# An adaLN block with routed attention on one core: a second set of slot orders, statistics spread over slots, keys of four heavy batches made early, and two banks for the last transposes

## The reference, cut to what matters

```
h = layernorm(x) * (1 + ca) + sa
x = x + ga * attention(h)                    # causal, one head of 128
h = layernorm(x) * (1 + cb) + sb
x = x + gb * ffn(h)
ffn(h):                                      # 8 heads of 64
    light = local_attention(rmsnorm(h))      # windows of 128 tokens, output projection
    s_q, s_kv = h @ q_token, h @ kv_token    # one score per token
    idx_q  = top 128 of 50 steps of coordinate descent on s_q
    idx_kv = top 256 of the same on s_kv
    q from rows idx_q, keys and values from rows idx_kv, values times their scores
    heavy = softmax(q k^T) v, projected, times the query scores
    return light, with heavy added at rows idx_q
```

## Time and profile before

| | us |
|---|---|
| median of 3 runs (480.55 to 482.89) | 482.2 |
| the profiled execution | 482.58 |
| its span, first to last instruction | 480.7 |
| PE busy | 445.8 (93%) |
| DVE busy | 328.1 (68%) |
| ACT busy | 345.6 (72%) |
| POOL busy | 267.3 (56%) |

### The profile page before, as it was taken

How to read it: one execution, slowest core, us unless ns; L and a number is a source line. 1 busy time by engine, 2 the same in 40 slices (tenths; PEclk the granted TensorE clock), 3 DMA queues, 4 the chain that set the end, 5 groups by cost and what they waited for, 6 DMA issues and landing times.

```text
span 480.7 us, 12054 instructions
## 1 busy us (share of the span) xinstructions
PE 445.8 (93%) x4088; PEld 393.3 (82%) x4088; DVE 328.1 (68%) x1099; ACT 345.6 (72%) x1260; POOL 267.3 (56%) x325
## 2 busy tenths in 40 slices
PE   7858889999999999899997799999999999999994
PEld 6747688998989988787786688888888888888873
DVE  5874788778768897989879964555555454555551
ACT  3665989889788877677775678667776766677761
POOL 3147576576576776332332335544666666556555
PEclk9996999999999999999999999999999999999998
DMA  6880000001001001000000000100000010000002
GB/s 219 237 314 22 14 13 13 13 1 33 25 1 35 23 20 49 3 12 13 12 12 13 6 8 24 35 18 7 12 11 13 12 18 14 16 12 13 7 8 22
DMA packets 20108, 16.28 MB, mean 34 GB/s; under 512 B 1968, under 2 KB 18880, under 8 KB 19792
## 3 DMA queue, kind: packets, MB, share of 16 engines
q1 hardware_dynamic: 16480, 13.01, 8.8%
q0 software_dynamic: 2816, 2.10, 3.3%
q10 hardware_dynamic: 752, 0.40, 0.3%
HBM read 10.23 MB, written 5.28 MB: 32 GB/s over the span
## 4 chain that ended last, share of the span: by engine, by line
PE 64%; DVE 14%; ACT 5%; issue 4%; POOL 4%; POOLq 0%; ACTq 0%; DVEq 0%
PE bank L905 6%; PE bank L916 6%; PE bank L660 6%; PE bank L931 6%; PE bank L662 5%; PE bank L661 5%; PE bank L813 4%; PE bank L854 4%; PE bank L843 4%; PE bank L827 4%; ACT pr L591 3%; PE bank L872 3%; DVE cd_min L1208 3%; PE bank L944 3%; DVE nmx L1162 2%
## 5 line engine op out<-in xcount | busy, mean ns | idle before, releaser
L420 POOL TENSOR_TENSOR pr<-pr,rinv 128x512 f32<-128x512 f32 x64 | 66.5, 1040 | 84.2 <-DVE rinv L1168 84.2
L432 POOL TENSOR_TENSOR pr<-pr,rinv 128x512 f32<-128x512 f32 x64 | 72.7, 1155 | 63.8 <-DVE rinv L1313 63.8
L591 ACT ACTIVATE pr<-bank,nmx 128x128 f32<-128x128 f32 x256 | 90.5, 377 | 20.8 <-DVE nmx L1162 20.7
L634 ACT ACTIVATE pr<-bank,nmx 128x256 f32<-128x256 f32 x128 | 59.3, 485 | 19.3 <-DVE nmx L1307 19.3
L1307 DVE TENSOR_REDUCE nmx<-bank 128x2 f32<-128x512 f32 x64 | 41.9, 681 | 33.4 <-PE bank L905 33.4
L644 ACT ACTIVATE pt<-bank 128x512 f32<-128x512 f32 x64 | 38.2, 596 | 27.0 <-PE bank L916 27.0
L591 ACT ACTIVATION_READ_ACCUMULATOR pr<-bank,nmx 128x1 f32 x256 | 55.5, 217 | 0.0
L1162 DVE TENSOR_REDUCE nmx<-bank 128x4 f32<-128x512 f32 x64 | 42.8, 672 | 8.5 <-PE bank L813 8.4
L827 PE MATMUL bank<-ident,pr 128*128 128x128 f32 x256 | 38.9, 275 | 7.4 <-POOL pr L420 6.8
L916 PE MATMUL bank<-ident,pr 128*128 128x128 f32 x256 | 38.8, 274 | 1.6 <-ACT pt L644 1.6
L827 PEld LDWEIGHTS bank<-ident,pr 128*128 128x128 f32 x256 | 29.6, 141 | 10.6 <-POOL pr L420 8.5
(11 more groups left out here) (218 smaller groups left out, 1315.8 us busy)
## 6 DMA issues: line engine op xcount, KB each, us to landing
mod_bc<-mod_rows_scratch SPq DMA_DIRECT2D x1, 2560.0 KB, 15.4
X<-in_L_attn_x SPq DMA_DIRECT2D x4, 512.0 KB, 8.0
xh_scratch<-xhs SPq DMA_DIRECT2D x16, 128.0 KB, 1.9
out<-X SPq DMA_DIRECT2D x16, 128.0 KB, 1.8
mod_bc<-mod_rows_scratch SPq DMA_DIRECT2D x1, 1024.0 KB, 7.8
wkv_raw<-in_L_ffn_wkv_light SPq DMA_DIRECT2D x1, 512.0 KB, 7.6
mod_bc<-mod_rows_scratch SPq DMA_DIRECT2D x1, 512.0 KB, 3.8
wmod_sb<-in_L_wmod ACTq DMA_DIRECT2D x1, 384.0 KB, 5.3
```

The costliest lines, as they stand in the source:

```text
L420: pool.tensor_tensor(q, q, rinv[u][:, :, None].broadcast_to([P, 4, P]), ALU.mult)\
L432: pool.tensor_tensor(q, q, rinv[u][:, 0:2, None].broadcast_to([P, 2, N]), ALU.mult)\
L591: act.activation(pr[u][:, i * P:(i + 1) * P], ps[bank][:, i * P:(i + 1) * P], ACT.Exp, bias=nmx[u][:, i:i + 1], accum_out=sums[u][:, i:i + ...
L634: act.activation(pr[u][:, i * N:(i + 1) * N], ps[bank][:, i * N:(i + 1) * N], ACT.Exp, bias=nmx[u][:, i:i + 1], accum_out=sums[u][:, i:i + ...
```

## The change

In the first 18 slots each engine but SP now walks a list of its own (`HEAD = 18`); the list for the other slots is changed too. `A_AT` is written out with the same numbers. In the second list most H entries of PE, ACT and DVE keep their order inside the slot.

The statistics of one batch are taken per slot, in slots 3 to 6, 13 to 16 and 22 to 25; the small operations follow in the last slot of each four, 1/std one slot after that and the bias two. `h_transpose` of batch 4 is preceded by eight `keep_busy` transposes.

The keys of heavy batches 0 to 3 are made in slots 67 to 74, one half (six matmuls) a slot, into bank 5; ACT copies them into rows of `mod_bc` that are no longer read. Both stand first in their slot. The projections and both evacuations of these batches in phase H go, and their scores read `mod_bc`.

For the last heavy batch units 1 and 3 are transposed into bank 1 and copied out by DVE; units 0 and 2 stay with bank 4 and ACT. Its reciprocal of unit 3 stands ahead of the evacuation of the batch before. POOL's scatter moves from lag 19 to lag 17 and behind the last `normalise_h` in its slot.

```diff
-A_AT = [5 * b // 2 for b in range(B)]
+A_AT = [0, 2, 5, 7, 10, 12, 15, 17, 20, 22, 25, 27, 30, 32, 35, 37]
+HEAD = 18
-def run_slots(stages):
+def run_slots(head, stages=None):
     for t in range(END):
-        for phase, lag, f, *unit in stages:
+        for phase, lag, f, *unit in head if t < HEAD or stages is None else stages:
...
-        STATS_AT = (4, 11, 19)
+        STATS_AT = (3, 13, 22)
+        KEPT = 4
+        KEPT_AT = [SCORES_AT + 18 + i for i in range(2 * KEPT)]
+        LAST_PT_BANKS = (4, 1)
...
-                       ("H", 1, gather), ("A", 11, xhat), ("A", 7, ln2_rstd), ("H", 19, scatter), ("L", 15, add_light),
+                       ("H", 17, scatter), ("L", 3, normalise, 0)])
...
+            def kept_evac(t):
+                if t in KEPT_AT:
+                    n = KEPT_AT.index(t)
+                    act.wait_ge(hv["keptp"], n + 1)
+                    act.activation(mod_bc[:, 2 * n:2 * n + 2, 0:2, :].rearrange("p c j d -> p c (j d)"),
+                                   ps[5][:, :].rearrange("p (c t) -> p c t", c=2), ACT.Copy).then_inc(hv["kept"], 1)
             def k_evac_h(b):
-                act.wait_ge(hv["kp"], 2 * b + 1)
+                if b < KEPT:
+                    return
+                act.wait_ge(hv["kp"], 2 * (b - KEPT) + 1)
...
             def pt_evac_h(b, u):
+                if b == B - 1 and u % 2:
+                    return
...
-                if b in (0, 2):
+                if b in (0, 2, 4):
                     keep_busy(8)
...
+            def project_kept(t):
+                if t in KEPT_AT:
+                    n = KEPT_AT.index(t)
+                    pe.wait_ge(a["xlo"], B)
+                    at_least(pe, hv["kept"], n)
+                    project_half(5, KH_w, n % 2, n // 2).then_inc(hv["keptp"], 1)
             def project_kh_0(b):
+                if b < KEPT:
+                    return
...
             def p_transpose_h(b, u):
+                bank = 4
+                if b == B - 1:
+                    bank = LAST_PT_BANKS[u % 2]
+                    if u % 2:
+                        at_least(pe, hv["PTd"], u // 2)
+                    else:
+                        pe.wait_ge(hv["PT"], 4 * b + u // 2)
...
             def late_stats(t):
-                if t in STATS_AT:
-                    stats1(1 + STATS_AT.index(t))
-                    mean_var1(1 + STATS_AT.index(t))
+                for n, first in enumerate(STATS_AT):
+                    if first <= t < first + 4:
+                        b = 4 * (n + 1) + t - first
+                        stats1(b, b + 1)
+                    if t == first + 3:
+                        mean_var1(n + 1)
...
+            def pt_evac_last(b, u):
+                if b == B - 1:
+                    dve.wait_ge(hv["PTp"], 4 * b + u + 1)
+                    dve.wait_ge(hv["Op"], b)
+                    dve.tensor_copy(pt[u][:, :], ps[LAST_PT_BANKS[1]][:, :]).then_inc(hv["PTd"], 1)
```

More of the change, by code:

```diff
@@ L231, in adaln_routed_attention @@
         hv = {n: sem("h_" + n) for n in (
[L232 to L233 removed]
+            "xg0", "xg1", "keptp", "kept", "xqp", "xq", "qp", "q", "kp", "ka", "kd", "vp", "v", "Sp", "mx", "p", "ri", "pn",
+            "PTp", "PT", "PTd", "Op", "oT", "outp", "fin", "out0", "out1")}
         block = ctx.enter_context(nc.Block())
@@ L894, in scores_h, with keys @@
                 pe.wait_ge(hv["q"], b + 1)
-                pe.wait_ge(hv["ka"], b + 1)
-                pe.wait_ge(hv["kd"], b + 1)
+                if b == 0:
+                    pe.wait_ge(hv["kept"], 2 * KEPT)
+                    pe.wait_ge(lt["vd"], B)
+                if b < KEPT:
+                    at_least(pe, hv["v"], 2 * b)
+                else:
+                    pe.wait_ge(hv["ka"], b - KEPT + 1)
+                    pe.wait_ge(hv["kd"], b - KEPT + 1)
+                def keys(rows, c):
+                    if b < KEPT:
+                        return mod_bc[rows, 4 * b + c, 0:2, :].rearrange("p j d -> p (j d)")
+                    return KT[b % 2][rows, c, :]
                 for n in range(2):
@@ L905, in scores_h @@
                             mm = pe.matmul(ps[SCORE_BANKS[n][i]][:, m * N:(m + 1) * N], QT[b % 2][rows, c, 0:NQ],
-                                           KT[b % 2][rows, c, :], start=True, stop=True)
+                                           keys(rows, c), start=True, stop=True)
                     mm.then_inc(hv["Sp"], 1)
@@ L913, in p_transpose_h @@
                     pe.wait_ge(lt["oTd"], B)
-                at_least(pe, hv["PT"], g)
+                bank = 4
+                if b == B - 1:
+                    bank = LAST_PT_BANKS[u % 2]
+                    if u % 2:
+                        pe.wait_ge(hv["xq"], B)
+                        at_least(pe, hv["PTd"], u // 2)
+                    else:
+                        pe.wait_ge(hv["PT"], 4 * b + u // 2)
+                else:
+                    at_least(pe, hv["PT"], g)
                 for i in range(4):
-                    mm = pe.transpose(ps[4][:, i * P:(i + 1) * P], pr[u][:, i * P:(i + 1) * P], ident[:, :])
+                    mm = pe.transpose(ps[bank][:, i * P:(i + 1) * P], pr[u][:, i * P:(i + 1) * P], ident[:, :])
                 mm.then_inc(hv["PTp"], 1)
@@ L939, in out_heavy @@
                 if b == 0:
-                    pe.wait_ge(a["xlo"], B)
+                    pe.wait_ge(hv["kept"], 2 * KEPT)
                     pe.wait_ge(woh_in, 16)
@@ L972, in mean_var, with stats1 @@
                 dve.tensor_tensor(ve, t[3], t[4], ALU.add).then_inc(seven, 1)
-            def stats1(i):
-                dve.wait_ge(x_in[i], 16)
-                for b in range(4 * i, 4 * i + 4):
+            def stats1(lo, hi):
+                dve.wait_ge(x_in[lo // 4], 16)
+                for b in range(lo, hi):
                     for q in range(C):
@@ L1313, in recip_h, with recip_late, recip_last @@
                 dve.reciprocal(rinv[u][:, 0:2], sums[u][:, 0:2]).then_inc(hv["ri"], 1)
+            def recip_late(b):
+                if b < B - 1:
+                    recip_h(b, 3)
+            def recip_last(b):
+                if b == B - 1:
+                    recip_h(b, 3)
             def o_evac_h(b):
```

132 lines of the change are left out of this document (84 added, 48 removed).

## The result

The changed kernel takes 479.79 us (median of 20 runs, the lowest 477.14) against 482.48 for the kernel before: a ratio of 0.9944, 95% interval 0.9927 to 0.9961, so 2.7 us faster. I had forecast 474.4, 7.8 us faster. The sign is right and the range held the time, but the gain is a third of the forecast.

A forecast was written before the change was run, and what follows sets the result against it. PE bounds the heavy stage and 75 to 200 us, DVE the selection beside the top-8 rounds. Terms -5.5 - 1.0 + 1.5 - 1.4 - 1.4 + 0 = -7.8 gave 474.8 from the profiled 482.58, stated as 474.4; range 469.0 to 480.5.

The forecast's parts named there:

- start, spreading and clock: Start to first light projection: transpose of batch 4 2.2 us sooner plus 3.3 from a full PE clock, together 5.5 us.
- second statistics block: At 59.35 us: splitting DVE's 2.5 us block into four pieces gains 1.0 us, between 0 and 2.5.
- lists elsewhere: New orders outside the other terms, mostly 75 to 200 us: little to win, 0, from -1.5 to +3 us.
- kept halves in the selection: Slots 67 to 74: eight added key halves, mostly hidden in PE's waits, cost 1.5 us, between 0 and 5.7.
- heavy stage: Phase H: removed key projections gain 0.45 us a batch, limited by P^T's bank; three gaps make 1.4 us.
- last batch: Last heavy batch: second P^T bank, earlier reciprocal and moved scatter gain 1.4 us, between 0.7 and 2.0.
- My first rival: Start: the clock falls all the same, amid short PE waits; only 2.2 of 5.5 us comes, 477.7 us; chance 0.18.
- rival 4: Start and light stages: lists bring other waits, a quarter of 6.5 us comes back, 479.3 to 482 us; chance 0.12.
- with no empty 4 us the clock should stay at 2.4 GHz: Start, 35 to 45 us: removing PE's long wait keeps the full clock, worth 3.3 of the 5.5 us.
- my sign of being right: Start: no PE wait above 1.5 us in 30 to 40 us and a clock of 1.00 until 45.
- rival 3: Phase H and selection: removed keys pay in full, added ones cost nothing, 468.6 us; chance 0.07.
- Rival 2: Selection: each kept half pays a whole round trip, 11 us in place of 1.5, 483.9 us; chance 0.08.

The follow-up runs named there:

- run 6: Run 5 plus 14 identity transposes on PE ahead of the last P^T of light batch 8: 479.73 us, ratio 0.9941 to the kernel before.
- Run 7: The kernel before, with only 30 identity transposes added ahead of the transpose of attention batch 4: 483.23 us, ratio 1.0008.
- run 2: The changed kernel with 27 more identity transposes on PE in four waits between 29 and 42 us: 478.04 us, ratio 0.9900 to the kernel before.
- run 8: The changed kernel with the last batch's four P^T in one bank again, all copied by ACT: 480.88 us, ratio 0.9984 to the kernel before.
- run 3: The changed kernel with no keys kept (KEPT = 0), waits of the kernel before put back: 482.68 us, ratio 0.998 to the kernel before.
- Run 10: run 9 with four instead of eight identity transposes ahead of the transpose of attention batch 4: 475.90 us, ratio 0.9876 to the kernel before.
- run 1: The changed kernel with the third statistics block one slot earlier (slots 21 to 24): 479.14 us, ratio 0.9942 to the kernel before.
- run 5: run 2 with POOL's power and DVE's last step for batches 12 to 15 three slots later (29 and 30): 480.75 us, ratio 0.9963.
- run 9: The changed kernel with the identity transposes of run 2 and run 6, third block's power in slot 27, DVE's step in 29: 476.11 us, ratio 0.9872.
- run 11: Run 10 with the seven followers of the second statistics block one slot later: 475.20 us, ratio 0.9853 to the kernel before.
- run 12: run 11 with no keys kept (KEPT = 0): 478.63 us, ratio 0.9929 to the kernel before.

## Why the prediction was wrong

| step | forecast | profiled | clock kept |
|---|---|---|---|
| start, spreading and clock | -5.5 | -0.65 | -3.85 |
| second statistics block | -1.0 | -0.45 | -0.45 |
| third block (in "lists elsewhere, 0") | 0 | +1.68 | +1.67 |
| rest of the lists | 0 | -0.25 | -0.24 |
| kept halves in the selection | +1.5 | +0.93 | 0.02 (run 6) |
| heavy stage | -1.4 | -1.04 | -1.01 (run 6) |
| last batch | -1.4 | -1.51 | -1.51 |
| sum | -7.8 | -1.3 | -5.4 |

The last column gives 482.5 - 5.4 = 477.1, which is where the executions at a clock of 0.996 begin (477.1); the one before it is the profiled pair of spans, 480.74 and 479.45. The measured 2.7 lies between. That my range held 479.79 is no merit of the sum: its upper part was there for rivals 1 and 4.

**The failed step is "with no empty 4 us the clock should stay at 2.4 GHz".** It stays in some executions and falls in others, though no wait in 30 to 40 us is above 1.5 us, as my sign of being right had it. My first rival named the cause, short waits in 35 to 40 us with PE busy little over half; I gave it 0.18. Run 7's profile shows the clock falling behind such waits even with the long one filled, and run 2 that filling them keeps it; between the changed kernel's profile and run 2's that is 3.06 us by the first light scores. Why it stays in some executions with the waits unfilled (run 8) stays open. The argument that I set against the rival was that the long gap is gone, and it looked at the gap and not at the waits that it had hidden. The Trainium skill (TensorE: Matmul & The Clock Gate, A second HAM failure mode: psum-queue depth-cycling) tells of clock swings from many short idles between groups of matmuls; I set against it that the selection showed none. The start of the changed kernel agrees in kind: three waits of 0.66 to 1.25 us, and a fall among them. My counterargument was too narrow: in the selection the clock fell behind single waits of 1.7 to 1.9 us, near 204 us in the changed kernel and near 261 and 278 us in run 3.

**Mis-sized in the same step:** with the clock kept the start gives 3.85, not 5.5. In run 8's profile the first light projection comes 3.89 us earlier than the 46.23 of the earlier trace rows:

```profile
42.34 0.36 PE L684 MATMUL bank<-XT_hi,Q_w_lo 128*128 128x256 f32 x1
```

Its transpose of batch 4 starts at 33.28, 1.64 earlier, where I had 2.2; the other 2.25 are the clock's, where I had 3.3. I had left 0.8 us to steps that no PE clock shortens. From that transpose to the first light projection PE's waits for ACT and DVE are 3.20 us in run 8 and 1.31 in the kernel before: at the full level PE waits 1.9 us more.

The transpose is later than I said for this reason: in the changed kernel the values' bias was done at 33.0 (32.59 and 0.41 long), not 32.2, since the first steps ran 0.9 us later than before (the scores of batch 3 at 30.15, before at 29.23); the identity transposes then held the transpose of batch 4 until 33.64. Run 10, with four of them, shows that this last part is worth nothing by the first light scores.

**The step that I costed at nothing, "the lists elsewhere",** cost 1.7 us between light batches 1 and 3. I followed the pieces of the second block and let the third go with "little to win and something to lose"; the something was a 1.65 us power ahead of rows that PE waits for, with DVE waiting for it in its order. Its price is within the +3 that I kept as the end. Runs 1 and 5 moved it and paid elsewhere; run 9 removed all but 0.3 us of it (19.11 and 17.19, in the kernel before 18.99 and 17.00). It is of the kind that rival 4 described, at about a third of its price.

**The second block** gave 0.45 of the 1.0, because its followers still stood ahead of the values' bias; run 11 gave 0.79 by moving them.

**Kept halves:** 1.5 was too much. Between light batch 8 and the heavy stage they cost 0.02 against the kernel before, 0.33 against run 12. That they fill waits behind which the clock falls is a gain that no term of mine had; without the clock they are worth 0.7 us (1.02 less 0.33).

**Right:** the heavy gap's bound (10.22 and the round trip of 1.43) and so rival 3's fall. That POOL's product ends within 0.1 us of the copy and would by itself hold P^T 2 nearly as long (argued from its end, not tested) is luck, for the sum did not have it. 0.92 of 1.4 came in the gaps, batch 1 giving only 0.08 since its query projection came 0.33 us later behind its first scores than before (it waits 0.21 us for DVE's values), and 0.1 more in the small drift of the later batches. The last batch was right in size, in its P^T 3 and in its cause (run 8). Rival 2 fell: the selection did not grow by more than a fall of the clock.

## What to carry to other kernels

Where, as here, an engine's clock falls behind its waits, a removed wait is not yet a kept clock: list the waits that come behind it, and fill them with work that nobody waits for, in places that are idle anyway. A small step that is moved takes its followers along, and a follower on an engine that runs ahead in its own list stalls all that is queued behind it; look for two places, one for the step and one for its reader, with the time of the step between them. When a cure moves a loss without shrinking it, the price is in the order, and the row just behind the new place names it.

## What the runs showed of the hardware

The same instructions with the same work in 35 to 40 us (PE busy 2.77 and 2.78 us of 5) saw the clock fall behind it in one execution and stay in the other, and so did the 2.11 us in 200 to 204 in the kernel after and before. What decides between the two was not found. What a fall costs differs by place: 3.2 us by the first light scores, 0.9 between light batches 9 and 10, though DVE is busy 3.8 to 3.9 us of 4 in those windows, and 1.2 near 270 us in run 12. With these waits filled (run 11) the executions lie within 0.9 us of each other, where those of the changed kernel spread over 6 (the one of 1512 us aside).
